# Recurrence with joined lower parts, first MLP layer in pairs with row-tiled half passes, mixing divided between the pairs

## The reference

```python
w = windows of 7x7 tokens of gn(x)            # 1024 windows, 49 tokens, 192 channels
w = layernorm(w, ln1)
h_t = w_t @ Bm + h_(t-1) @ A                  # t = 0..48, the recurrence over a window's tokens
xr = h @ Cm                                   # the mixing
y = gelu(layernorm(xr, ln2) @ W1 + b1) @ W2 + b2      # W1: 192 x 768, W2: 768 x 192
x = x + xr + y
```

## Time and profile before

| what | value |
|---|---|
| median of 3 runs | 4611.31 us (4606.82 to 4611.5) |
| the profiled execution | 4597.89 us, span 4596.1 us |
| TensorE matmul busy | 4316.2 us, 94% |
| VectorE busy | 3933.2 us, 86% |
| ScalarE busy | 2476.2 us, 54% |
| GpSimd busy | 2584.1 us, 56% |
| mean granted TensorE clock | 0.987 of full |

### The profile page before, as it was taken

One profiled execution on the slowest core, in us unless ns is written; L12 is line 12 of the kernel. 1 busy time (PEld: TensorE's weight loads), 2 busy tenths in 40 slices (PEclk: granted clock), 3 DMA queues, 4 the chain that ended last, 5 costly groups with the idle time before them and its releaser, 6 DMA issues. The chain is left out here.

```text
span 4596.1 us, 142253 instructions
## 1 busy us (share of the span) xinstructions
PE 4316.2 (94%) x52232; PEld 3688.3 (80%) x52232; DVE 3933.2 (86%) x8105; ACT 2476.2 (54%) x4852; POOL 2584.1 (56%) x2092
## 2 busy tenths in 40 slices
PE   0599999999999999999995999999999999999998
PEld 0488888888888888888885888888888888888887
DVE  6698888888888888888872888888888888888888
ACT  0244444444444444444441666777776766776676
POOL 1155555555555555555542666666666666666666
PEclk9999999999999999999996999999999999999999
DMA  8011111111111111111111222222222222222222
GB/s 354 17 39 39 39 39 39 39 39 39 40 41 39 39 39 39 39 39 39 39 34 46 71 76 74 75 74 74 74 76 75 75 75 75 74 74 74 74 74 69
DMA packets 389849, 286.06 MB, mean 62 GB/s; under 512 B 147147, under 2 KB 388091, under 8 KB 388603
## 3 DMA queue, kind: packets, MB, share of 16 engines
q1 hardware_dynamic: 387060, 283.20, 21.2%
q10 hardware_dynamic: 2736, 2.14, 0.1%
HBM read 120.39 MB, written 87.31 MB: 45 GB/s over the span
## 5 line engine op out<-in xcount | busy, mean ns | idle before, releaser
L892 POOL TENSOR_TENSOR L<-L,mx 128x588 f32<-128x588 f32 x512 | 600.3, 1172 | 644.0 <-DVE mx L1118 643.9
L603 PE MATMUL ps_o<-w,g_hi 128*128 128x384 f32 x2352 | 711.1, 365 | 5.9 <-DVE g_lo L543 4.1
L415 ACT ACTIVATE gF<-ps_g,b1f 128x512 f32<-128x512 f32 x588 | 404.7, 688 | 392.9 <-PE ps_g L634 390.8
L886 POOL TENSOR_TENSOR E<-E,ri 128x588 f32<-128x588 f32 x512 | 600.0, 1172 | 0.8 <-DVE ri L1124 0.8
L1180 PE MATMUL ps_s<-Kp,Q 32*64 32x98 f32 x12288 | 494.5, 259 | 59.9 <-DMA Kp<-K 58.8
L603 PE MATMUL ps_o<-w,g_lo 128*128 128x192 f32 x2352 | 535.0, 255 | 0.0
L442 POOL TENSOR_TENSOR res<-xt,b2b 128x768 f32<-128x768 f32 x98 | 181.1, 1848 | 591.2 <-DVE x L491 591.2
L401 ACT ACTIVATE h_hi<-ps_h,hbias 128x512 fp32r<-128x512 f32 x196 | 123.1, 679 | 703.7 <-PE ps_h L618 703.7
L1114 DVE SCALAR_TENSOR_TENSOR L<-ps_s,bias 128x588 f32<-128x588 f32 x512 | 394.6, 771 | 92.2 <-PE ps_s L1180 76.5
L603 PEld LDWEIGHTS ps_o<-w,g_hi 128*128 128x128 f32 x2352 | 429.9, 189 | 26.8 <-issue 24.8
L999 ACT ACTIVATE o_hi<-ps_v,vb 128x98 fp32r<-128x98 f32 (+1 forms) x1024 | 289.1, 334 | 300.5 <-PE ps_v L1293 293.3
(11 more groups left out here) (222 smaller groups left out, 12495.5 us busy)
## 6 DMA issues: line engine op xcount, KB each, us to landing
xs<-in_x SPq DMA_DIRECT2D x8, 4704.0 KB, 22.2
xt<-in_x SPq DMA_DIRECT2D x98, 384.0 KB, 3.4
x_cells<-x SPq DMA_DIRECT2D x784, 48.0 KB
xb<-x_cells SPq DMA_DIRECT2D x128, 294.0 KB
Vx<-V SPq DMA_DIRECT2D x512, 73.5 KB
out<-yo SPq DMA_DIRECT2D x128, 294.0 KB
Kp<-K SPq DMA_DIRECT2D x256, 98.0 KB, 2.0
Kp<-K SPq DMA_DIRECT2D x256, 49.0 KB, 1.9
```

The lines of the kernel that those rows point to most:

```text
L415: act.activation(gF[f % 4][:, :], ps_g[:, f % 2, :], ACT.Gelu, bias=b1f[:, f:f + 1]).then_inc(s_gelu, 1)
L603: last = pe.matmul(dst, g[:, f, P * k:P * (k + 1)], w, start=(f == 0 and i == 0), stop=(f == FT - 1 and i == 1))
L886: pool.tensor_tensor(e, e, ri[p][:, :].unsqueeze(2).to_broadcast([P, HEADS, T]), ALU.mult)\
L892: pool.tensor_tensor(l, l, mx[p][:, :].unsqueeze(2).to_broadcast([P, HEADS, T]), ALU.subtract).then_inc(s_sub, 1)
```

## The change

The recurrence joins the two lower passes of the b rows. A new weight tile `W_AB_b_lo` holds W_B's b_lo in rows 0 to 63 and W_A's in rows 64 to 127, and a new data tile `xh_b` holds xn's b upper part and h's b upper part in the same rows, both copied by ScalarE. Each output block of the recurrence takes 9 passes in place of 10.

The first layer works on blocks in pairs. Four whole passes for each block of a pair, then for both the fifth one with only 64 rows: block f in array rows 0 to 63, block f+1 in rows 64 to 127, from a copy `y_b` of y's b upper part that ScalarE makes. Both blocks of a pair release `s_w1` there. The mixing (state times C) of the four token tiles is no longer behind the first layer: two tiles stand behind the first pair, two behind the second.

ScalarE has three more copies in a slot: y_b behind y_hi, h's behind the MLP's g_hi, xn's behind xn_hi. In the prologue VectorE makes `W_AB_b_lo`, GpSimd leaves out the two b_lo of A and B, and GpSimd has two more memsets at the stage's start.

```diff
                     pool.wait_ge(s_wh, 1)
                     for full, parts in ((fold_B, W_B), (raw_A, W_A), (raw_C, W_C), (fold_1, W_1)):
-                        for t in range(2):
+                        for t in range(1 if parts in (W_A, W_B) else 2):
...
+                    dve.wait_ge(s_wh, 1)
+                    for full, parts, rows in ((fold_B, W_B, slice(0, CB)), (raw_A, W_A, slice(CB, P))):
+                        dve.tensor_tensor(W_AB_b_lo[rows, :], full[rows, 1, :], parts.parts[2][rows, :], ALU.subtract)
                     dve.wait_ge(s_sum, 1)
...
                         act.wait_ge(s_t2, n + 1)
                         upper_parts(y_hi, ps_g).then_inc(s_yh, 1)
+                        act.wait_ge(s_yh, n + 1)
+                        act.activation(y_b[CB:P, :], y_hi[0:CB, 1, :], ACT.Copy).then_inc(s_yb, 1)
...
+                    if there(n + 1):
+                        act.wait_ge(s_hh, n + 2)
+                        act.activation(xh_b[1 - c][CB:P, :], h_hi[1 - c][0:CB, 1, :], ACT.Copy).then_inc(s_hs, 1)
                     if there(n + 2):
                         act.wait_ge(s_t1, n + 3)
                         upto(act, s_scan, n + 1)
                         upper_parts(xn_hi[c], ps_h).then_inc(s_xh, 1)
+                        act.wait_ge(s_xh, n + 3)
+                        act.activation(xh_b[c][0:CB, :], xn_hi[c][0:CB, 1, :], ACT.Copy).then_inc(s_xs, 1)
...
+                    pool.memset(xh_b[c][:, :].bitcast(fp32), 0.0)
...
                         pe.wait_ge(s_xl, n + 2)
+                        pe.wait_ge(s_xs, n + 2)
                         upto(pe, s_hl, n)
+                        upto(pe, s_hs, n)
                         for m, rows in enumerate((P, CB)):
                             cols = slice(P * m, P * m + rows)
-                            terms = (*W_B.terms(xn_hi[d], xn_lo[d], cols), *W_A.terms(h_hi[d], h_lo[d], cols))
+                            terms = (*W_B.terms(xn_hi[d], xn_lo[d], cols)[0:4], *W_A.terms(h_hi[d], h_lo[d], cols)[0:4],
+                                     (W_AB_b_lo[:, cols], xh_b[d][:, :]))
...
                         pe.wait_ge(s_yl, n + 1)
-                        for f in range(FT):
-                            if f >= 2:
-                                pe.wait_ge(s_gelu, FT * n + f - 1)
-                            terms = W_1.terms(y_hi, y_lo, slice(P * f, P * (f + 1)))
-                            for k, (w, v) in enumerate(terms):
-                                last = pe.matmul(ps_g[:, f % 2, :], w, v, start=(k == 0), stop=(k == len(terms) - 1))
-                            last.then_inc(s_w1, 1)
-                    if there(n + 1):
-
-                        d = 1 - c
-                        pe.wait_ge(s_hl, n + 2)
-                        upto(pe, s_y, n + 1)
-                        upto(pe, s_rsum, n + 1)
-                        for k in range(TPC):
-                            terms = W_C.terms(h_hi[d], h_lo[d], slice(0, C), lambda v: v[:, P * k:P * (k + 1)])
-                            for i, (w, v) in enumerate(terms):
-                                last = pe.matmul(tok_tile(ps_r, k), v, w, start=(i == 0), stop=(i == len(terms) - 1))
-                        last.then_inc(s_cm, 1)
+                    for f in range(0, FT, 2):
+                        if there(n):
+                            for g in (f, f + 1):
+                                if g >= 2:
+                                    pe.wait_ge(s_gelu, FT * n + g - 1)
+                                terms = W_1.terms(y_hi, y_lo, slice(P * g, P * (g + 1)))[0:4]
+                                for k, (w, v) in enumerate(terms):
+                                    pe.matmul(ps_g[:, g % 2, :], w, v, start=(k == 0), stop=False)
+                            pe.wait_ge(s_yb, n + 1)
+                            w = W_1.parts[3]
+                            pe.matmul(ps_g[:, 0, :], w[0:CB, P * f:P * (f + 1)], y_hi[0:CB, 1, :],
+                                      start=False, stop=True).then_inc(s_w1, 1)
+                            pe.matmul(ps_g[:, 1, :], w[CB:P, P * (f + 1):P * (f + 2)], y_b[CB:P, :],
+                                      start=False, stop=True).then_inc(s_w1, 1)
+                        if there(n + 1) and f < TPC:
+
+                            d = 1 - c
+                            if f == 0:
+                                pe.wait_ge(s_hl, n + 2)
+                                upto(pe, s_y, n + 1)
+                                upto(pe, s_rsum, n + 1)
+                            for k in (f, f + 1):
+                                terms = W_C.terms(h_hi[d], h_lo[d], slice(0, C), lambda v: v[:, P * k:P * (k + 1)])
+                                for i, (w, v) in enumerate(terms):
+                                    last = pe.matmul(tok_tile(ps_r, k), v, w, start=(i == 0), stop=(i == len(terms) - 1))
+                            if f == 2:
+                                last.then_inc(s_cm, 1)
```

More of the change, by code:

```diff
@@ L105, in build @@
             W_B, W_A, W_C = (Split(ctx, name, C) for name in ("wB", "wA", "wC"))
+            W_AB_b_lo = sb("wAB_b_lo", [P, C], f32r)
             W_1 = Split(ctx, "w1", HID)
@@ L281, in build @@
             yb = sb("yb", [P, TPC, C])
+            xh_b = [sb(f"xh_b{b}", [P, NTOK], f32r) for b in range(2)]
+            y_b = sb("y_b", [P, NTOK], f32r)
             y_hi, y_lo = sb("y_hi", [P, 2, NTOK], f32r), sb("y_lo", [P, NTOK], f32r)
@@ L314, in build @@
             s_t1, s_xh, s_xl = sem("xn_transposed"), sem("xn_hi_ready"), sem("xn_lo_ready")
+            s_xs, s_hs = sem("xn_b_hi_stacked"), sem("h_b_hi_stacked")
             s_scan, s_hh, s_hl = sem("scan_summed"), sem("h_hi_ready"), sem("h_lo_ready")
@@ L318, in build @@
             s_rs2, s_y = sem("ln2_rstd"), sem("y_ready")
+            s_yb = sem("y_b_hi_repeated")
             s_t2, s_yh, s_yl = sem("y_transposed"), sem("y_hi_ready"), sem("y_lo_ready")
```

## The result

The changed kernel takes **5047.9 us** (median of 4 runs, 5043.9 to 5054.3) against 4609.1 us (4 runs, 4606.3 to 4611.5) of the kernel before: a ratio of 1.0955, 95% interval 1.0940 to 1.0971. It is slower by 439 us. The forecast was 4940 us in a range of 4800 to 5060: the sign and the mechanism came out, the size was 108 us short.

A forecast was written before the change was run, and what follows sets the result against it. The first stage was taken as bound by two tied loops of 22.79 us, TensorE's and the stores'. 4611 us plus 245 (tail, 98 x 2.50) plus 83 (clock, 98 x 0.85) gave 4939, say 4940; range 4800 to 5060.

The forecast's parts named there:

- The tied loops: First stage: TensorE's loop and the stores-and-load loop tie at 22.79 us; less TensorE work alone would give nothing.
- The recurrence: Recurrence on TensorE: loses two of 20 passes, -0.46 us a slot.
- The tail: From first to second layer: ScalarE's and VectorE's work behind the last pair delays the second layer by 2.96 us a slot.
- the pairs' term: First layer's half passes on row tiles: 0.26 us switch cost for a pair, against 0.23 saved.
- rival C: First layer: halves don't overlap or the switch is dearer; +314 us and the clock on top, 5010; chance 0.09.
- the main case: First stage: longer wait before the second layer, net +2.50 us a slot, with clock falls; 4940 us; chance 0.55.
- The walk without any switch cost: First-stage slot walked with row-tile switches free: +1.94 us a slot, 4801 us.
- The wait before the transposes: TensorE before the transposes of xn: a new wait of about 1.9 us, as VectorE's xn normalization ends late.
- The clock: TensorE's idle time in the first stage: falls in half the slots at 1.7 us, +0.85 a slot, +83 us.
- Rival A: First stage: the longer wait before the second layer without clock falls, 4856 us, between 4801 and 4876; chance 0.30.
- Rivals D and E: First-stage slot: TensorE's -1.15 us comes through, 4498, chance 0.04; or stores' loop holds 22.79, no change, 4611, chance 0.02.
- Edits at no cost: ScalarE's three copies and the prologue's edits lie in waits: 0, at most 2 us once for the prologue.

The follow-up runs named there:

- GpSimd beside g_lo: Kernel before with joined lower parts, xt load ahead of stores, GpSimd's x1 square and first accumulation ahead of the small power: 4941.9 us.

## Why the prediction was right, and where it was not

**The tied loops** were right in what they were used for: less TensorE work alone gives little (0.24% with the joined parts), more of it shows in full. But "two loops" was short by one. VectorE's own, with the collision on GpSimd, stood behind the stores' loop, and nothing in the prediction named it. It made no difference to the forecast, since TensorE's loop became the longest by far.

**The recurrence**, -0.46: measured -0.46.

**The tail** was walked at +2.96 and measured +3.49. The steps hold one by one: halves at 2.05 (walked 2.03), the first gelu after them at 2.59 (sums at 2.42), halves of the second pair at 5.62 (5.48), of the third at 9.24 (8.93), gelu 4 at 9.85 (9.37), g_lo 5 ready at 13.56 (13.03), second layer at 13.69 (13.16). Gelu 4's lag of 0.48 is the pairs' term, mis-sized: 0.49 for the halves with their switches was 0.61, which makes up 0.24 of the 0.31 by which the third halves are late, and the gelu follows them by 0.61 in place of 0.44, since a half pass lasts 0.50 and not 0.39. The upper bound of 0.26 for a switch was too low; the pair costs 0.38 more than its 0.23 of array time. 0.05 comes from g_lo's longer pair (1.37). Of rival C one half is out, the halves one behind the other: they start at 1210.82 and 1210.83. Its other half, a dearer switch, came true: the slot without the clock is 3.49 - 0.46 = 3.03 us longer, nearer to C's 3.2 than to the 2.50 of the main case, and C's 5010 is nearer to the measured time than 4940. The rows on small tiles were a poor measure of this switch. The walk without any switch cost is also off by a little: by its own steps it comes to +1.90, not +1.94. The Trainium skill, "TensorEngine Tiling (Array Packing)", section "Key Properties", says that a change of the tiling mode drains the engine; this trace agrees in that each change costs time, 0.09 us going in, and 0.19 and 0.09 coming out.

**The wait before the transposes** was forecast at 1.9 and is 0.56 (0.82 if counted, as the forecast was, from the end of the array time at 1218.24). VectorE's normalization of xn takes 2.22 us, not the 3.25 of the earlier trace rows, since only one of GpSimd's two g_lo runs beside it (1217.31 to 1218.59). The error went into the other wait, 2.30 in place of 1.1 to 1.2, and not into the sum: g_lo 5, not the transposes, comes last.

**The clock** was the second mis-sized term. The price of a fall was near (1.7 forecast; 1.48 in the changed kernel, where some 0.2 us of the slow stretch lies in the wait, 1.6 in the one with only the mixing divided). The frequency wasn't: every slot, not every second. The half was a guess and not worked out from rows. Half of the slots is what the kernel with only the mixing divided has, with a wait of 1.93 before the second layer; the changed kernel has 0.56 and 2.30 about its transposes. The changed kernel's 98 x 1.48 = 145 stand against the 83 forecast; filling the wait gave 110 of them back. The forecast's upper bound, 2.2 a slot, held.

**The sum.** 98 x (3.49 - 0.46 + 1.48) = 442, where 328 was forecast. Of the 114 us between them, 98 x (3.49 - 2.96) = 52 belong to the pairs' cost and 98 x (1.48 - 0.85) = 62 to the clock; the forecast's rounding and the medians bring it to 108. Both terms were short, and the time lies only 12 us below the top of the range. Rival A (no falls, 4856) fell with the windows; with the tail as measured it would have been 4611 + 98 x 3.03 = 4908, and the kernel with filling passes, which keeps its clock, takes 4938, since it waits 0.4 us more in each slot before the first layer. Rivals D and E, which needed g_lo 5 by t0 + 9.3, miss by more than 4 us.

**Edits at no cost.** ScalarE's extra copies are in no wait list of TensorE, as expected. The scaling of xn takes 2.08 us beside GpSimd (1228.98, and 2.09 in the middle of its 98 times), more than the 1.38 + 0.2 that I allowed at worst; the delay by the clock hid it, and VectorE waits 1.04 us for h_hi behind it.

## What to carry to other kernels

Before work is moved or shortened on a full engine, walk the chain of the engine that feeds it next and ask what work covered its tail: here 2.2 us of mixing covered four ScalarE and two VectorE operations, and moving it together with the pairing cost three times what all the removed passes could be worth (3.49 against 1.15 us a slot), before the clock took 1.48 more. A full TensorE in a window says nothing on whether fewer passes pay; the small waits that come back in every slot do, and where several loops tie, each has to be shortened before any gain shows. Where one wait in each period can't be removed, work of no use in it can be cheaper than the fall of the clock.

## What the runs showed of the hardware

- **Falls settle into a pattern.** The same kind of wait gave falls in every slot (period 27.3 throughout), in about four of five (whole fifth passes; ScalarE by pairs), in about three of four (GpSimd beside g_lo), or in every second (24.82 and 26.4), and none in the kernel with the mixing behind, where the wait was 0.69 and two others 0.78. Why one pattern and not another was not settled, and the length of the wait alone doesn't order them: every slot with 2.30 (and 0.56 before the transposes), four of five with 2.11 (and 0.52) and with 2.33, three of four with 2.83, every second with 1.93.
- **A fall has one length, not one place.** In 2 us windows the granted clock adds up to 3.4 us at the lower level each time: 0.56 and 0.58 in the changed kernel, 0.56 and 0.59 with only the mixing divided, 0.60 and 0.54 with whole fifth passes, 0.74, 0.50 and 0.91 with ScalarE by pairs. It begins about 0.2 us before TensorE resumes in the first of these and 1.3 us after in the second (resumed at 1210.92, slow from about 1212.2).
- **VectorE beside GpSimd took 2.2 and 3.3 times as long** where both read SBUF: 4.17 us for two g_lo in place of 1.28, 2.08 to 2.19 for the scaling of xn in place of 0.96. In the first case VectorE and GpSimd together were done in 4.25 us (1204.97 to 1209.22), 0.36 under what x1's square, one accumulation and the two g_lo need one after another (1.47 + 1.86 + 1.28 = 4.61). The Trainium skill, "SBUF — State Buffer", section "Who interferes with whom", says that a VectorE instruction with two inputs in SBUF contends with a GpSimd instruction that reads SBUF; these numbers agree with it. The normalization of xn, which reads one tile, shows it too: 3.25 us beside two of GpSimd's g_lo, 2.22 beside one, 1.24 beside none (the kernel with ScalarE by pairs). Whoever moves a load or a GpSimd operation moves that collision.
- **Two half passes on row tiles** start 0.01 us apart and share the array, but last 0.50 us where a whole pass in a row lasts 0.39 (the first whole pass of a group shows 0.50 too). With three switches in and three out, the six half passes of a slot cost 0.56 us more than six whole ones, where 0.69 less was on offer.
